# A two-layer tanh recurrence on one core: layer 0 moved to the split-bank form of layer 1, residual sums moved to GpSimd

## The reference

```python
def layer(x, h0, Wx, Wh, b):
    xW = einsum('ntd,dh->nth', x, Wx) + b
    h_t = tanh(h_{t-1} @ Wh + xW_t)      # a scan over t, h_{-1} = h0
    return all h_t

x = x + layer(x, cond, L0_Wx, L0_Wh, L0_b)
x = x + layer(x, cond, L1_Wx, L1_Wh, L1_b)
```

## Time and profile before

| what | value |
|---|---|
| time, median of 3 runs | 2185.19 us (2184.86 to 2185.83) |
| time of the profiled execution | 2181.98 us |
| its span on the core | 2180.2 us |
| PE busy | 2157.1 us (99%), 90304 records |
| DVE busy | 1306.2 us (60%) |
| ACT busy | 807.7 us (37%) |
| POOL busy | 8.6 us |

### The profile page before, as it was taken

The page is one execution under the profiler, slowest core; times in us unless marked ns, Lnnn a source line. Parts: engine busy times, 40 slices in busy tenths (PEclk is TensorE's granted clock), DMA queues, the critical chain, the costliest instruction groups (busy, mean ns, idle before and its releaser), DMA issues.

```text
span 2180.2 us, 192439 instructions
## 1 busy us (share of the span) xinstructions
PE 2157.1 (99%) x90304; PEld 2127.9 (98%) x90304; DVE 1306.2 (60%) x5643; ACT 807.7 (37%) x3585; POOL 8.6 (0%) x11
## 2 busy tenths in 40 slices
PE   7999999999999999999999999999999999999997
PEld 7999999999999999999999999999999999999997
DVE  3566666666666666666666666666666666666665
ACT  2333333333333333333333333333333333333333
POOL 1000000000000000000000000000000000000000
PEclk9999999999999999999999999999999999999999
DMA  3000000000000000000000000000000000000000
GB/s 101 23 26 22 26 22 26 22 26 22 26 22 26 22 26 22 26 22 26 22 26 22 26 22 26 22 25 23 24 23 25 23 25 23 24 24 23 25 22 17
DMA packets 112033, 55.84 MB, mean 26 GB/s; under 512 B 12448, under 2 KB 111024, under 8 KB 111536
## 3 DMA queue, kind: packets, MB, share of 16 engines
q1 hardware_dynamic: 111456, 53.53, 8.5%
q10 hardware_dynamic: 432, 1.18, 0.1%
q0 software_dynamic: 32, 0.02, 0.0%
HBM read 37.90 MB, written 16.78 MB: 25 GB/s over the span
## 4 chain that ended last, share of the span: by engine, by line
PE 99%; DVE 0%; DMA 0%; issue 0%; ACT 0%; SPq 0%; DVEq 0%; ACTq 0%
PE ps L221 41%; PE ps_rec L238 21%; PE ps_rec L249 16%; PE ps L210 10%; PE ps_xw L210 10%; DMA wx<-wx_in 0%; DVE zt L391 0%; DVE z L397 0%; ACT h L331 0%; DVE zt L387 0%; ACT h L324 0%; SPq L180 0%; SPq L178 0%; DVE h L405 0%; DVEq L53 0%
## 5 line engine op out<-in xcount | busy, mean ns | idle before, releaser
L221 PE MATMUL ps<-wh,h 128*32 128x128 f32 x32768 | 1089.6, 273 | 4.9 <-ACT h L324 2.8
L221 PEld LDWEIGHTS ps<-wh,h 128*32 128x32 f32 x32768 | 907.9, 110 | 22.9 <-ACT h L324 5.1
L238 PE MATMUL ps_rec<-wh,h 128*32 128x128 f32 x16384 | 638.8, 273 | 7.8 <-ACT h L331 7.1
L391 DVE STREAM_TRANSPOSE zt<-ps_rec 128x128 f32<-128x128 f32 x1024 | 324.6, 317 | 423.2 <-PE ps_rec L249 417.0
L405 DVE TENSOR_TENSOR h<-h 128x16 f32<-128x16 f32 x2050 | 359.4, 175 | 354.4 <-ACT h L331 319.1
L249 PE MATMUL ps_rec<-wh_part,h 128*32 128x128 bf16 x24576 | 534.2, 219 | 0.9 <-issue 0.8
L324 ACT ACTIVATE h<-zt 128x32 f32<-128x32 f32 x1024 | 235.1, 230 | 725.1 <-DVE zt L387 725.1
L238 PEld LDWEIGHTS ps_rec<-wh,h 128*32 128x32 f32 x16384 | 463.1, 110 | 14.8 <-ACT h L331 13.4
L331 ACT ACTIVATE h<-z 128x32 f32<-128x32 f32 x1024 | 235.1, 230 | 637.4 <-DVE z L397 637.4
L249 PEld LDWEIGHTS ps_rec<-wh_part,h 128*32 128x32 bf16 x24576 | 460.2, 97 | 2.7 <-issue 1.6
L210 PE MATMUL ps<-wx,x_pe 128*32 128x128 f32 x8192 | 414.7, 273 | 4.8 <-ACT ps L306 3.0
(11 more groups left out here) (21 smaller groups left out, 22.7 us busy)
## 6 DMA issues: line engine op xcount, KB each, us to landing
x_pe<-x_t SPq DMA_DIRECT2D x256, 64.0 KB, 2.0
x_dve<-x_t SPq DMA_DIRECT2D x256, 64.0 KB, 2.0
out_t<-x_out SPq DMA_DIRECT2D x256, 64.0 KB, 1.5
wx<-wx_in SPq DMA_DIRECT2D x4, 256.0 KB, 8.0
wh<-wh_in ACTq DMA_DIRECT2D x1, 1024.0 KB, 8.6
wh<-wh_in SPq DMA_DIRECT2D x1, 1024.0 KB, 4.7
wx<-wx_in SPq DMA_DIRECT2D x1, 1024.0 KB, 8.2
bias<-b_in ACTq DMA_DIRECT2D x2, 64.0 KB, 4.0
```

What stands on the lines that cost most here:

```text
L221: mm = pe.matmul(rows(ps0[n // S4 % 2], g), h_step(0, n - 1)[:, k, :], wh[0][:, k, g * P:(g + 1) * P], start=False, stop=k == KC - 1, skip ...
L238: pe.matmul(rows(bank, g), h_step(1, n - 1)[:, k, :], wh[1][:, k, g * P:(g + 1) * P], start=False, stop=False, skip_group_check=True, tile ...
L391: dve.transpose(zt[1][n % 2][:, :], ps_rec1[n % 2][:, 0:P]).then_inc(zt1_done, 1)
```

## The change

Layer 0 takes the form of layer 1, with one of its four tiles in bf16 parts (`KB = (1, 2)`; the first 8 steps keep all four in float32, `PARTED`). It gets banks of its own for the recurrence, `begin`, `total` and the two `rest` subtractions. VectorE's order is rewritten so that the steps of the two layers interleave; the second subtraction of a layer stands behind the transposition of the other layer. ScalarE's order is tanh, begin, tanh, begin. The residual sums go to GpSimd, and `sum_mid`, `sum_out` now wait for rec_done. One tile of layer 0's projection is moved one half slot earlier, and SyncE issues the x_pe load ahead of the store.

```diff
-KB = 2
+KB = (1, 2)
-WARM = 8
+WARM = 6
+PARTED = RING
-PROJECT = (((0, 0), (0, 1)), ((0, 2), (1, 0)), ((1, 1), (1, 2)), ((1, 3), (0, 3)))
+PROJECT = (((0, 1), (0, 2)), ((0, 3), (1, 0)), ((1, 1), (1, 2)), ((1, 3), (0, 0)))
...
+            def recur(l, n):
+                bank = ps_rec[l][n % 2]
+                whole = range(KC) if l == 0 and n < PARTED else range(KB[l], KC)
+                if n:
+                    pe.wait_ge(*h_count(l, n - 1))
...
+                for k in whole:
+                    for g in range(QG):
+                        mm = pe.matmul(rows(bank, g), h_step(l, n - 1)[:, k, :], wh[l][:, k, g * P:(g + 1) * P],
...
+                if is_split(l, n - 1):
+                    pe.wait_ge(*split_count(l, n - 1))
...
+                for k in range(whole.start):
+                    for i in range(PARTS):
+                        for g in range(QG):
...
-            pool.wait_ge(s_wh[1], DMA)
+            for l in LAYERS:
+                pool.wait_ge(s_wh[l], DMA)
...
+            def sum_mid(c):
+                pool.wait_ge(x_dve_loaded[c % 2], DMA * (c // 2 + 1))
+                if c >= 2:
+                    pool.wait_ge(out_done, c - 1)
+                if c == NG - 1:
+                    pool.wait_ge(h_last, 1)
+                else:
+                    pool.wait_ge(rec_done, STEP_AT[0, S4 * (c + 1)])
+                pool.tensor_tensor(x_group(x_mid, c), x_group(x_dve, c), h_group(0, c), ALU.add).then_inc(mid_done, 1)
...
+            def sum_out(c):
...
+                    pool.wait_ge(rec_done, STEP_AT[1, S4 * (c + 1)])
+                pool.tensor_tensor(x_group(x_out, c), x_group(x_mid, c), h_group(1, c), ALU.add).then_inc(out_done, 1)
...
+            for c in range(NG + 2):
+                if c >= 2:
+                    sum_out(c - 2)
+                if c < NG:
+                    sum_mid(c)
...
             def slot(s):
+                n0, n1, before = number(0, s), number(1, s), number(1, s - 1)
+                if n0 is not None:
+                    turn(0, n0)
+                if before is not None:
+                    rest_second(1, before)
+                if n0 is not None:
+                    lower(0, n0)
+                    total(0, n0)
+                    rest_first(0, n0)
+                if n1 is not None:
+                    turn(1, n1)
+                if n0 is not None:
+                    rest_second(0, n0)
+                if n1 is not None:
+                    lower(1, n1)
+                    total(1, n1)
+                    rest_first(1, n1)
```

More of the change, by code:

```diff
@@ L132, in h_count, with is_split, split_count @@
             return h_done[s // S4 % 2], steps.index((l, s)) + 1
-        def split_count(n):
-            s = n + LAG
-            return split_done[s // S4 % 2], s % S4 + 1
+        def is_split(l, n):
+            return (n >= 0 if l else n >= PARTED - 1) and n < T - 1
+        def split_count(l, n):
+            s = n + LAG * l
+            steps = [t for t in range(s - s % S4, s + 1) if is_split(l, t - LAG * l)]
+            return split_done[l][s // S4 % 2], len(steps)
         block = ctx.enter_context(nc.Block())
@@ L187, in _ @@
             for c in range(1, NG + 4):
+                if 2 <= c + 1 < NG:
+                    sp.wait_ge(proj_done[0], c)
+                    load(x_pe, x_pe_loaded, c + 1)
                 if c >= 4:
@@ L427, in slot @@
[L427 to L442 removed]
+                                  AX.X, ALU.add).then_inc(z_done[l], 1)
@@ new lines, in rest, with rest_first, rest_second @@
+            def rest(l, n, part):
+                step, to, of, tiles = h_step(l, n), h_cols(n, part), h_cols(n, part - 1), slice(0, KB[l])
+                return dve.tensor_tensor(step[:, tiles, to], step[:, tiles, of], h_bits(l, n)[:, tiles, of],
+                                         ALU.subtract)
+            def rest_first(l, n):
+                if is_split(l, n):
+                    dve.wait_ge(*h_count(l, n))
+                    rest(l, n, 1).then_inc(rest_done[l], 1)
+            def rest_second(l, n):
+                if is_split(l, n):
+                    dve.wait_ge(rest_done[l], n + 1 if l else n + 2 - PARTED)
+                    rest(l, n, 2).then_inc(split_count(l, n)[0], 1)
@@ new lines, in lower @@
+            def lower(l, n):
+                if (n + LAG * l) % S4 == 0 and is_split(l, n - 1):
+                    done, count = split_count(l, n - 1)
+                    dve.sem_inc(done, -count)
+            def slot(s):
+                n0, n1, before = number(0, s), number(1, s), number(1, s - 1)
[15 more added lines that the diff above has]
+                    rest_first(1, n1)
@@ L456, in _ @@
             dve.wait_ge(s_hinit, 2)
-            rest(-1, 1).then_inc(s_hrest, 1)
+            rest(1, -1, 1).then_inc(s_hrest, 1)
             dve.wait_ge(s_hrest, 1)
-            rest(-1, 2).then_inc(s_hsplit, 1)
-            for s in range(T + LAG + 1):
+            rest(1, -1, 2).then_inc(s_hsplit, 1)
+            for s in range(T + LAG):
                 slot(s)
```

241 lines of the change are left out of this document (90 added, 151 removed).

## The result

The changed kernel takes 2276.58 us (median, 2275.34 to 2281.86) where the kernel before took 2185.07 us beside it: ratio 1.042, 95% interval 1.0405 to 1.0441. That is +91.5 us; the forecast was +63 and 2248 us, in a range of 2190 to 2312. The profiled execution took 2275.34 us, its span 2273.5.

The account below looks back on a forecast made before the run. TensorE's issued work was taken as the bound, at 2.08 us a slot. 1016 x (-0.05 + 0.05 + 0.06) = +61, plus 2.4 for the head, gave +63 us: 2248 by the median, range 2190 to 2312.

Parts of the forecast that it names:

- split wait: TensorE waits for layer 1's second subtraction, queued behind layer 0's transposition, before the bf16 parts: 0.05 us in every slot.
- late sums: GpSimd's two sums delay layer 1's tanh, making layer 0's next transposition 0.235 us late each fourth slot, 0.06 per slot.
- put at nothing: Priced at zero: layer 0's begins on ScalarE, GpSimd's four more preparations, the earlier x_pe load, the moved projection tile.
- Tile in parts: One tile of layer 0 in bf16 parts saves TensorE 0.05 us in each of 1016 slots, alone -51 us.
- rival (c): TensorE doesn't wait for the split (chain under 0.66) and a sum is under 0.30: 2137 us; chance 6%.
- Other loops: Layer 0's load comes at E + 1.16, needed at E + 1.21; VectorE's round of 2.00 stays under 2.08: both hold.
- head: First 8 slots, layer 0 alone on its own chain: transposition to tanh grows by 0.30 us, +2.4 us in all.
- Rival (a): GpSimd's sums and VectorE's subtractions exclude each other, delaying sum_mid 0.07 us per fourth slot: +18 us, 2266; chance 25%.
- (b): Sums short or early enough: at 0.25 us each, only 0.006 per slot and the head remain, about 2194 us; chance 10%.
- the second wait of `tanh1`: On ScalarE, a tanh that waits on two semaphores starts 0.37 us after the total in place of 0.30, 0.07 more.

Follow-up runs that it names:

- The two pairs of kernels: Layer 0 all in float32: 2329.44 us against the change's 2276.58; 2215.13 against 2146.46 with sums between VectorE's subtractions and two ScalarE waits moved.
- the freed form: The change with sums placed between VectorE's subtractions and x_mid awaited by TensorE a slot later: 2155.98 us; with two ScalarE waits moved too, 2146.46.
- a memset: The changed kernel with each GpSimd sum replaced by a memset of 420 scratch columns that reads nothing: 2261.8 us, ratio 1.035.
- the gain of the gaps: Against the change, sums placed between VectorE's subtractions and the wait for x_mid moved from layer 1's tanh to TensorE: 2155.98 us, ratio 0.987.
- the last kernel: Two tiles of layer 0 in bf16 parts in place of one, against the 2146.46 us kernel: 2108.28 us, ratio 0.965 to the kernel before.

## Why the prediction came out as it did

Slower was right, 2276.58 lies in the range, and the place was right: `tanh1` of each fourth slot behind `sum_out` and `sum_mid`. The point value is 28 us short: the split wait was 41 us too much (0.01 per slot for 0.05), the late sums 65 us too little ((2.537 - 2.041) x 254 = 126 for 61), and 9 us came from what was put at nothing. That makes 33. The two errors were large and mostly cancelled, so that the point came so near is in good part luck.

- **Tile in parts, -0.05 per slot:** right. Layer 0's step takes TensorE 0.873 in float32 and 0.655 + 0.167 with the tile in parts, 0.051 less. The two pairs of kernels give 53 and 69 us, for reasons of their own in part (above).
- **Split wait, +0.05 per slot:** measured 0.01, so 41 us too much. The piece that failed is the subtraction at 0.175. Queued behind the transposition, the second subtraction takes 0.13; the load follows 0.05 after its end, as forecast, and TensorE's first part starts at 1006.74, 0.66 after E = 1006.08, just when TensorE gets there. What is left is that the first weights no longer come ahead: in the kernel before they were loaded 0.107 before their matmul, now 0.003, and layer 1's 24 instructions in parts take 0.345 in place of 0.335. The hundreds of equals that spoke against rival (c) were all subtractions that had waited, the first for the tanh and the second for the first; none had stood queued behind another instruction, as the second one does now. The mean of such a group was good to 0.05 only for its own kind of start.
- **Late sums, +0.06 per slot:** measured 0.50 per fourth slot, or 0.125 per slot; the forecast had 0.235 per fourth slot. Each piece was small: start 0.34 for 0.30, a sum 0.455 for 0.36 and that twice, hand-over 0.13 for 0.10, the last step 0.04 as forecast. They add to 1.41 where 1.155 was forecast. Of the 0.26, 0.19 is the sum's length, for which I took the middle of 0.25 and 0.47, and the upper end was right. The row of 1024 elements gave a slope of 1.75 ns where 2.1 was measured, and the row of one element a fixed part of 0.10 where it is 0.18: that row is a memset with nothing to read, and stood for an instruction with two inputs.
- **At nothing:** wrong for `begin` of layer 1 and for the wait for x_pe. The page after has the former at 104 us of waiting for the projection, of which the kernel before has no row. Both hold a tanh on ScalarE, and with VectorE's round at 2.00 against a slot of 2.04 little takes that back: slots of 2.07, and 9.5 us shown by moving them in the freed form.
- **Other loops, head:** right. Of 280 waits of a float32 tile for a tanh, 254 are those of the fourth slots; the head took 2.2 us for 2.4.
- **Rival (a):** the mechanism is real, the price in the change wrong. I gave it +18 for a delay of `sum_mid`. But GpSimd was first at the shared place, and VectorE's subtraction was drawn out (0.35), beside a tanh that was late anyway. It cost nothing: without any drawn-out subtraction the chain from `sum_out` to the next transposition is as long (1.429 with layer 0 in float32, 1.428 in the change), and so is the hand-over between the sums, 0.133. Where the mechanism decides is the kernel with the sums released earlier, 0.25 and more per fourth slot. The Trainium skill (SBUF — State Buffer, "SBUF: two separate sides") says that the two exclude each other and that whoever starts first keeps the port; the traces agree, with 0.35 and 0.40 for a subtraction of 0.13 and 0.17, and with none drawn out beside a memset. Who is first does not quite follow the recorded starts: 0.027 behind the sum's start the subtraction still went first, 0.064 behind it no longer.
- **Rivals (b), (c):** with the sums cut to 0.20 the time is 2163, under the 2194 of (b), since the split wait of (b) was nearly absent too. Those are the conditions of (c), and its 2137 is 26 too low: 10 of the split's 0.01, 9 of the two waits priced at nothing, and 7 of the second wait of `tanh1` in the fourth slot (2.069 for 2.041) make it up.
- The Trainium skill (GPSIMD Engine Reference, "Performance versus the Vector engine"), by its 2.2 ns per element, put a sum at an estimated 0.38; the traces agree with its slope (2.1) and show a larger fixed part than I added to it.

What stays open: why a sum of GpSimd starts 0.026 later behind TensorE's step, and is handed over 0.025 later, than a memset. The stretched subtraction is not the reason, since both are the same where none is stretched. Open too are the two shares in the gain of the gaps, and the bound of the last kernel.

## What to carry to other kernels

Work moved from an engine that bounded nothing can still land in a chain that does: before moving it, list what waits for its result, and get it out of that wait, by an earlier start or by a wait that stands later. The same two sums cost 114 us with the tanh of their slot waiting for them, and nothing once TensorE waited for them a slot later and they lay in the gaps of the engine that they exclude. Price an instruction on an engine that has none like it by the upper bound when it stands twice in a chain, and read whether the instructions behind a mean had waited or stood queued before that mean decides over 0.05.

## What the runs showed of the hardware that was not expected

- A two-input float32 instruction of GpSimd over 128 partitions took 0.200 us for 8 elements and 0.455 for 128. A memset of 420 columns took 0.448.
- A small subtraction of VectorE took 0.13 when it was queued behind other work and 0.17 when it had waited for ScalarE.
- A subtraction that started 0.06 to 0.13 after such a GpSimd instruction took 0.42 to 0.35 and ended 0.02 to 0.03 after it; behind it, the rest of VectorE's queue waits.
- TensorE's loop body of 24 slots cost 30% (2957 us against 2277) with instructions fetched anew on each turn, 13.22 MB against 0.39, at a mean granted clock of 0.958 of full speed; the body of 8 slots was not fetched again, and its branch adds some 0.04 us to a turn.
- Weights of TensorE that had to wait for the split came 0.003 us ahead of their matmul in place of 0.107, and that made 24 bf16 instructions take 0.345 us in place of 0.335.
